# A residual block of two 3x3 convolutions: x's planes by negation and accumulating DMAs, conv 2's difference plane in rounded passes

## The reference

```python
identity = x
out = jax.nn.relu(_bn(_conv3x3(x, w1, stride=1), g1, b1, m1, v1))
out = _bn(_conv3x3(out, w2, stride=1), g2, b2, m2, v2)
return jax.nn.relu(out + identity)
```

## Time and profile before

| what | value |
|---|---|
| median of 3 runs | 596.51 us (595.66 to 597.7) |
| profiled execution | 596.25 us |
| its span, first to last instruction | 594.3 us |
| mean granted clock of TensorE | 0.994 of full speed |
| busy: TensorE, VectorE, ScalarE, POOL | 97%, 93%, 80%, 3% |
| DMA | 53.23 MB, mean 90 GB/s |
| one load of x, one store | 814 KB, 4.3 us to landing; 392 KB, 2.8 us |

### The profile page before, as it was taken

How to read it: one execution, slowest core, us unless ns; L and a number is a source line. 1 busy time by engine, 2 the same in 40 slices (tenths; PEclk the granted TensorE clock), 3 DMA queues, 4 the chain that set the end, 5 groups by cost and what they waited for, 6 DMA issues and landing times.

```text
span 594.3 us, 8667 instructions
## 1 busy us (share of the span) xinstructions
PE 576.5 (97%) x2962; PEld 533.7 (90%) x2962; DVE 555.3 (93%) x475; ACT 472.6 (80%) x730; POOL 19.8 (3%) x28
## 2 busy tenths in 40 slices
PE   6769999999999999999999999999999999999997
PEld 3769999999999999999999999999999999999996
DVE  6899999999999999999999999999999999999963
ACT  5687888887788887788887778888778888778874
POOL 7500000000000000000000000000000000000000
PEclk9799999999999999999999999999999999999999
DMA  4112223322223331232332222332122233121012
GB/s 161 56 61 88 104 84 110 112 82 82 83 83 110 110 108 56 83 109 84 110 110 67 89 92 83 110 110 93 71 83 93 100 110 110 58 82 51 29 55 108
DMA packets 22458, 53.23 MB, mean 90 GB/s; under 512 B 1584, under 2 KB 18096, under 8 KB 22448
## 3 DMA queue, kind: packets, MB, share of 16 engines
q1 hardware_dynamic: 22304, 52.80, 25.0%
q10 hardware_dynamic: 144, 0.29, 0.2%
HBM read 27.40 MB, written 25.69 MB: 89 GB/s over the span
## 4 chain that ended last, share of the span: by engine, by line
PE 93%; DVE 2%; ACT 1%; issue 0%; POOL 0%
PE psum L639 93%; DVE x_outer L367 1%; DVE x_lo L375 1%; DVE psum L389 1%; ACT w_mat L488 0%; DVE t_outer L412 0%; POOL g_t L181 0%; ACT psum L514 0%; DVE t_inner L398 0%; DVE x_inner L355 0%; ACT out_sb L563 0%; ACT z L534 0%; ACT z L535 0%; DVE x_inner L359 0%
## 5 line engine op out<-in xcount | busy, mean ns | idle before, releaser
L639 PE MATMUL psum<-x_hi,w_hi 128*128 128x392 f32 (+2 forms) x512 | 175.3, 342 | 6.7 <-DVE x_lo L375 6.7
L639 PE MATMUL psum<-x_hi,w_lo 128*128 128x392 f32 (+2 forms) x512 | 175.8, 343 | 0.0
L639 PE MATMUL psum<-x_lo,w_hi 128*128 128x392 f32 (+2 forms) x512 | 175.1, 342 | 0.0
L389 DVE TENSOR_TENSOR psum<-psum,z 128x784 f32<-128x784 f32 (+1 forms) x128 | 127.1, 993 | 21.3 <-ACT hidden L540 9.9
L639 PEld LDWEIGHTS psum<-x_hi,w_hi 128*128 128x128 f32 x512 | 97.0, 189 | 8.3 <-issue 4.8
L639 PEld LDWEIGHTS psum<-x_hi,w_lo 128*128 128x128 f32 x512 | 97.0, 189 | 0.4
L639 PE MATMUL psum<-t_inner,w_mat 128*128 128x392 f32 x256 | 94.7, 492 | 2.7 <-ACT psum L514 2.7
L639 PEld LDWEIGHTS psum<-x_lo,w_hi 128*128 128x128 f32 x512 | 97.0, 189 | 0.4
L563 ACT ACTIVATE out_sb<-psum 128x784 f32<-128x784 f32 x64 | 52.8, 825 | 47.1 <-PE psum L639 47.0
L639 PE MATMUL psum<-h_lo,w_hi 128*128 128x392 f32 x256 | 87.3, 341 | 0.0
L639 PE MATMUL psum<-h_hi,w_hi 128*128 128x392 f32 x256 | 87.2, 341 | 0.0
(11 more groups left out here) (67 smaller groups left out, 747.5 us busy)
## 6 DMA issues: line engine op xcount, KB each, us to landing
x_sb<-x_dram SPq DMA_DIRECT2D x32, 814.0 KB, 4.3
out_dram<-out_sb SPq DMA_DIRECT2D x64, 392.0 KB, 2.8
w_raw<-w_dram ACTq DMA_DIRECT2D x1, 288.0 KB, 3.5
w_raw<-w_dram SPq DMA_DIRECT2D x1, 288.0 KB, 5.4
bn<-params_dram SPq DMA_DIRECT2D x1, 132.0 KB, 3.7
```

The source lines that it names most:

```text
L389: nc.vector.tensor_tensor(psum[:, half, EVEN:ODD + 1, 0:width], t1, z[:, half, :, 0:width], ALU.add).then_inc(joined[conv], 1)
L639: ins = nc.tensor.matmul(psum[:, half, bank, first:first + (j1 - j0) * WQ], w[:, i, far, :], moving, start=not onto and at == 0, stop=at = ...
```

## The change

- **Planes of x.** VectorE no longer adds and subtracts planes of x. `negate_x(s + 2)` writes minus the even columns into the second inner plane, and minus the columns one further into both outer planes, as two `tensor_scalar` instructions, two images ahead. A plain DMA (`load_even`) puts the even columns in the first inner plane. POOL issues two accumulating DMAs an image, which add x from DRAM: the odd columns to both inner planes (`add_inner`), the other operand to the outer planes (`add_outer`). The planes keep the padding column (29 columns a row instead of 28: 812 elements a plane), `x_outer` has two buffers, and x is loaded two steps further ahead.
- **Conv 2's difference plane** is split like the others: `split_hidden("inner", ...)` and `high_hidden("inner", ...)` now take both inner planes (1624 elements instead of 812), and its products are three rounded passes. TensorE waits for `hlo_ready["inner"]` ahead of both inner products, where it waited for the raw difference plane ahead of the first.
- **Zero rows** above and below x's planes are gone; conv 1's matmuls leave them out as before. The scratch of the filters lies in `z` and `out_sb`.
- The loop of steps is one turn shorter, and more steps stand outside it.

```diff
+            def load_even(n, k):
+                sp.dma_start(x_inner[:, k, 0], x_rows[n][:, 0:RUN]).then_inc(even_in[k], 16)
...
             def step(s, k):
-                if not isinstance(s, int) or s + 2 < N:
-                    wait(sp, tx_ready["outer"], s + 3 - XBUFS)
-                    load(sp, s + 2, k + 2)
+                if not isinstance(s, int) or s + 4 < N:
+                    wait(sp, negated["outer"], s + 3)
+                    load(sp, s + 4, k + 4)
                 if there_is(s, s - 2):
                     store(s - 2, 0)
                     store(s - 2, 1)
+                if not isinstance(s, int) or 0 <= s < N - 3:
+                    wait(sp, res_ready, 2 * s)
+                    load_even(s + 3, (k + 3) % 4)
...
+            def add_inner(n, k):
+                pool.wait_ge(even_in[k], (n - k) * (16 // TBUFS) + 16)
+                pool.wait_ge(negated["inner"], n + 1)
+                odd = x_rows[n][:, XPLANE + 1:XPLANE + 1 + RUN].unsqueeze(1).broadcast_to((P, 2, RUN))
+                pool.dma_start(x_inner[:, k], odd, accum_op=ALU.add).then_inc(tx_ready["inner"][k % 2], 16)
+
+            def add_outer(n, k):
+                pool.wait_ge(negated["outer"], n + 1)
+                pool.dma_start(x_outer[:, k % 2], runs(x_rows[n], 0, XPLANE),
+                               accum_op=ALU.add).then_inc(tx_ready["outer"][k % 2], 16)
+
+            add_inner(0, 0)
+            add_outer(0, 0)
...
             scale_matrix(pool, "all2")
-            low_weights(pool, "all2")
+
+            def step(s, k):
+                if is_step(s, 0):
+                    low_weights(pool, "all2")
+                if there_is(s, s + 2):
+                    add_inner(s + 2, (k + 2) % 4)
+                    add_outer(s + 2, (k + 2) % 4)
...
+            def negate_x(n, k):
+                dve.wait_ge(x_in[k % XBUFS], until(n, k))
+                wait(dve, res_ready, 2 * (n - TBUFS) + 2)
+                cells = x_sb[:, k % XBUFS]
+                nc.vector.tensor_scalar(x_inner[:, k, 1], cells[:, 0:RUN], -1.0, None,
+                                        ALU.mult).then_inc(negated["inner"], 1)
+                wait(dve, xlo_ready["outer"], n - 1)
+                nc.vector.tensor_scalar(x_outer[:, k % 2], runs(cells, 1, XPLANE), -1.0, None,
+                                        ALU.mult).then_inc(negated["outer"], 1)
+
+            negate_x(0, 0)
...
-                if ahead:
-                    sum_x(s + 1, ka)
-                if last:
-                    split_hidden("t1", s - 1, kl % 2)
-                if ahead:
-                    difference_x(s + 1, ka)
+                if there_is(s, s + 2):
+                    negate_x(s + 2, (k + 2) % 4)
+                if last:
+                    split_hidden("inner", s - 1, kl % 2)
                 if now:
                     join(1, s, 1, (2, s - 2))
-                if ahead:
-                    outer_x(s + 1, ka)
                 if last:
                     split_hidden("outer", s - 1, kl % 2)
...
-                if (conv, i) == (2, 2):
-                    return ((t_inner[:, 1], wmat[2]),)
...
-                elif i == 1:
-                    hi, lo = t1_hi, t1_lo
+                elif i in (1, 2):
+                    hi, lo = ti_hi[:, i - 1], ti_lo[:, i - 1]
...
-                pe.wait_ge(th_ready["t2"], n + 1 + more)
+                pe.wait_ge(hlo_ready["inner"], n + 1 + more)
                 pe.wait_ge(res_ready, 2 * n + half + 1)
                 sum_products(2, half, 2, SUM_T2, passes_of(2, 2, 0), True).then_inc(inner[2], 1)
-
-                pe.wait_ge(hlo_ready["t1"], n + 1 + more)
                 sum_products(2, half, 1, SUM_T1, passes_of(2, 1, 0), True).then_inc(inner[2], 1)
```

More of the change, by code:

```diff
@@ L65, in residual_block, with scratch @@
         out_sb = sb("out_sb", [P, 2, 2, (NQ // 2) * WQ])
-        w_raw = {1: sb("w1_raw", [P, 3, 3, C]), 2: sb("w2_raw", [P, 3, 3, C])}
+        spare = {1: z[:].rearrange("p h s r -> p (h s r)"), 2: out_sb[:].rearrange("p h s r -> p (h s r)")}
+        def scratch(conv, at, kinds):
+            size = kinds * 3 * C
+            return spare[conv][:, at:at + size].rearrange("p (k h c) -> p k h c", k=kinds, h=3)
+        w_raw = {conv: scratch(conv, 0, 3) for conv in (1, 2)}
         bn = sb("bn", [P, 8 + 4 * C])
@@ L75, in residual_block @@
         bias = sb("bias", [P, 2])
[L76 to L77 removed]
+        g_t = {conv: scratch(conv, 9 * C, 4) for conv in (1, 2)}
+        g_sum = {conv: scratch(conv, 21 * C, 1)[:, 0] for conv in (1, 2)}
         wmat = {1: sb("w1_mat", [P, 4, 2, P]), 2: sb("w2_mat", [P, 4, 2, P])}
@@ L144, in run @@
                 step(s, s % 4)
-            with eng.Fori(0, (N - 4) // 4) as turn:
+            with eng.Fori(0, (N - 8) // 4) as turn:
                 for k in range(4):
                     step(turn * 4 + (2 + k), (2 + k) % 4)
-            for s in range(N - 2, N + 2):
+            for s in range(N - 6, N + 2):
                 step(s, s % 4)
@@ L230, in newton_step, with runs, until @@
             after(eng.tensor_tensor(inv[:, part], inv[:, part], tmp[:, part], ALU.mult))
[L232 to L238, removed]
+        def runs(cells, first, step):
+            return cells[:, first:first + 2 * step].rearrange("p (s r) -> p s r", s=2)[:, :, 0:RUN]
         def x_full(which, k):
-            full, places = (x_outer[:], slice(0, 2)) if which == "outer" else (x_inner[:, k], slice(2, 4))
-            return full.rearrange("p s j q -> p s (j q)"), places
+            full, places = (x_outer[:, k % 2], slice(0, 2)) if which == "outer" else (x_inner[:, k], slice(2, 4))
+            return full.rearrange("p s (j c) -> p s j c", c=WQ + 1)[:, :, :, 0:WQ], places
         def x_part(t, k, places):
-            return t[:, k % 2, places, 1:NQ + 1, :].rearrange("p s j q -> p s (j q)")
+            return t[:, k % 2, places]
+        def until(n, k):
+            return (n - k % 2) * 8 + 16
         def hidden_rows(half):
@@ L254, in hidden_parts @@
             rows = hidden_rows(half)
-            if which == "t1":
-                return t_inner[:, 0, rows], t1_hi[:, rows], t1_lo[:, rows]
+            if which == "inner":
+                return t_inner[:, :, rows], ti_hi[:, :, rows], ti_lo[:, :, rows]
             return t_outer[:, :, rows], h_hi[:, b, :, rows], h_lo[:, b, :, rows]
@@ L298, in _ @@
             nc.gpsimd.memset(wmat[1][:], 0.0).then_inc(mat_zeroed, 1)
-            for t in (x_hi, x_lo):
-                for b in range(2):
-                    for row in (0, NQ + 1):
-                        nc.gpsimd.memset(t[:, b, :, row, :].bitcast(F32), 0.0).then_inc(zeroed, 1)
             nc.gpsimd.memset(hidden[:], 0.0).then_inc(zeroed, 1)
             nc.gpsimd.memset(wmat[2][:], 0.0).then_inc(mat_zeroed, 1)
+            def add_inner(n, k):
[9 more added lines that the diff above has]
+            add_outer(0, 0)
             after, row = chain(pool, bn_step[2]), slice(2 + C, 2 + 2 * C)
@@ L522, in high_hidden @@
                 act.wait_ge(th_ready[which], n + 1 + (half or 0))
-                wait(act, *((inner[2], 4 * n) if which == "t1" else (outer[2], 2 * (n - 1))))
+                wait(act, *((inner[2], 4 * n) if which == "inner" else (outer[2], 2 * (n - 1))))
                 nc.scalar.activation(hi, full, ACT.Copy).then_inc(hhi_ready[which], 1)
```

83 lines of the change are left out of this document (41 added, 42 removed).

## The result

| | before | after |
|---|---|---|
| median of the runs beside each other | 596.09 us | **697.66 us** |
| profiled execution, span | 596.25, 594.3 us | 698.68, 697.0 us |
| mean granted clock of TensorE | 0.994 | 0.933 |
| DMA | 53.23 MB, 90 GB/s | 119.82 MB, 172 GB/s |

The ratio is 1.1687 (95% interval 1.1643 to 1.1731). The forecast was 656.5 us with a range of 638 to 699: the sign is right, the median lies just inside the range, and 40 us are missing from the sum. They have two causes, the start and TensorE's clock, and neither is in the term that the prediction worked on hardest.

The account below looks back on a forecast made before the run. It took TensorE's matmuls to bound the kernel before. Span 594.3 + 57.6 (ring) + 3.7 (start) - 1.0 (end) = 654.6 us; with 1.95 around the span and a correction to the median, 656.5 us, range 638 to 699.

Parts of the forecast that it names:

- Matmuls: Conv 2's difference plane: six rounded slots replace two true fp32 products in each half, saving 0.24 us, 0.48 us a step.
- The ring: TensorE, ReLU, VectorE, TensorE: conv 2 waits 2.38 us a step for both inner low parts; +57.6 us in all.
- Negations: VectorE's two negations ahead of the inner split handle two elements at a time: 0.50 and 0.91, together 1.41 us.
- Rival 2: VectorE's negations run at one element a cycle: 1.26 us more a step, 38 us in all, 694 us; chance 0.10.
- Rival 3: POOL's accumulate issue and VectorE's outer negation hold each other up: 2.0 us a step, 60 us more, 717 us; chance 0.10.
- Start: Image 1's accumulates land at 29.8 us; conv 2 begins at 42.7 instead of 39.03: +3.7 us (0 to 7).
- DMA: Plain and accumulating loads need 15.1 of a step's 19.5 us even at twice the plain price for accumulates: costed at nothing.
- Rival 4: Accumulates so slow that DMA engines bound the step; at four times the plain price 24.4 us, about 800; chance 0.06.
- Stores: SyncE's stores stand behind a wait for the negation, but the output buffer is needed a whole step later: nothing.
- End: The last step's splits are done before TensorE asks, so two images' matmul savings stand: -1.0 us.
- Rival 1: TensorE's matmuls stay the bound if the low parts come within 8.57 us of the step's start: 585 us; chance 0.06.
- the step of 19.54 us: The loop's period: 10.95 us from conv 1's to conv 2's inner products, then 8.59; 19.54 for 17.64, in 30 intervals.

Follow-up runs that it names:

- e10: e9 with SyncE issuing an image's first store ahead of the wait for the next load; 586.94 us, ratio 0.9857 to the kernel before.
- e3: The kernel before with only conv 2's difference plane in three rounded passes, x's planes still by VectorE's sums and differences; 639.03 us, ratio 1.0713.
- e4: The changed kernel with conv 2's difference plane again as one true fp32 pass, so only the planes' part of the change; 614.18 us, ratio 1.0299.
- e1: The changed kernel with VectorE's split of the inner hidden planes put ahead of the negations; 630.12 us, ratio 1.0568.
- e5: The changed kernel with 12 matmuls of 92 columns into unread PSUM columns where TensorE waits in each step; 671.13 us, ratio 1.1257.
- e2: e1 with ScalarE's output ReLU also moved ahead of the rounding of the inner hidden planes; 617.08 us, ratio 1.0361.
- e8: e2 with the planes of images 0 and 1 made by VectorE from x_sb, without accumulating DMAs; 599.58 us, ratio 1.005.
- e9: e8 with VectorE's hidden sum and difference ahead of the last join, and ScalarE's rounding ahead of the output ReLU again; 590.48 us, ratio 0.9904.

## Why the prediction was right, and where it was wrong

- **Matmuls, -0.48 us a step**: right. A rounded pair takes 1.06 us (six slots, 348.24 to 349.30), and e10's step comes within 0.06 to 0.23 us of 17.16.
- **The ring, +57.6 us**: right, in its mechanism and its size. The short steps are 19.48 to 19.57 us for 19.54; only 28 of the 30 intervals are such steps. TensorE's idle time reads 2.10 to 2.17 rather than 2.38, since a profile's modelled end of a matmul lies a little behind its slot. The rounded passes bring the wait (e3 has it, e4 does not), the order in front of the split sets its length (e1), and the DMAs have no part in it (e3 has none that accumulates).
- **Negations, 1.41 us**: right (0.49 + 0.91). Rival 2 fell. By the Trainium skill's "VectorE: DVE Perf Modes", section "Mode 2×_2P", such a form handles two elements a cycle; the trace agrees, with 812 elements in 0.57 us, where the two-source `TENSOR_TENSOR` of the earlier trace rows takes 1.00.
- **Rival 3, POOL and VectorE in each other's way**: it did not come. POOL's issue at 365.39 (1.20 us) overlaps the end of the outer negation, which takes 1.00, and the two issues run beside the split, which takes 1.84 as in the earlier trace rows. The Trainium skill's "SBUF — State Buffer", section "Who interferes with whom", would have one of them held for the other's whole length; between a negation and an issue in the loop, which overlap by only 0.3 us, the trace shows no such hold. At the start one inner negation (31.67 to 32.24) ran wholly inside the issue of 31.63 and took 0.57 us like all others; that issue took 1.76 us, and whether the negation made it longer is open.
- **Start, +3.7 us**: the step that failed, as a size. It was 19.0, outside my 0 to 7. I wrote "a load lands 4.3 us after issue", and took that for an accumulate; image 0's plane was rounded 13.5 us after its issue and image 1's 10.7 us. I had also shifted the end of POOL's filter work by 2 us, to 25.5, where it was 31.70: I had left out that ScalarE fills conv 2's matrix only behind the rounding of image 0's planes, and so behind their landing. That makes 12.5 of the 15.3 us that were missing. The other 2.8 lie behind TensorE's start on image 1: its outer accumulate landed 4.6 us behind the inner one, so that VectorE's outer split began at 48.44, 2.8 us after the inner one had ended. The nearest row had been a plain load on a quiet queue; two accumulates, the loads and the filters at once were the case at hand. The Trainium skill's "DMA: Bandwidth & Descriptors", section "Anatomy of one DMA — SWDGE (gpsimd) path", from which the estimate of 3.9 us came, gives less than any accumulate here took: the medians are 10.9 and 15.2 us, and the shortest in any run took 7.4.
- **The clock**: the term that was missing. Nothing in the prediction asked what a TensorE that stands still every step does to its own clock. It costs 27 us behind the first interval, of which e5 gives back 25.5.
- **DMA, "I cost it at nothing"**: right in the steady state by its cover, and nearer to the edge than I thought. An accumulate takes 0.402 x 697.0 / 53.22 = 5.3 us of all engines for 1 MB, a plain one in the same run 0.308 x 697.0 / 66.11 = 3.2 (2.8 before). My bound was twice the plain price; the DMA share is 0.76 to 0.79 in a step, and 15.1 of 19.5 is 0.77. Rival 4 fell.
- **Stores, nothing**: right for the changed kernel, whose steps are long, but thin: they land after 11.4 us instead of 2.8, and when the ring is shorter (e2, e8, e9) ScalarE waits for them.
- **End, -1.0 us**: right, -0.9.
- **Rival 1, TensorE stays the bound**: fell for this order of instructions; e10 is that rival with another order.

So the range held the median by 2.4 us, and for reasons that it had not been drawn for: its upper end stood there for slower negations and for rival 3, which did not come. That the forecast held is luck; the step of 19.54 us is not.

## What to carry to other kernels

When work leaves an engine, look at where in its order it stood: what counts is what stands between the ring's two ends, not the engine's busy share. Price a wait that you add to TensorE at its length and, as with the 2.15 us here, at the slower products that can follow it, and if it can't be removed, ask whether reordering two instructions shortens it before anything else is tried. And take no landing time from a quiet queue for a start in which everything is loaded at once.

## What the chip showed that I had not expected

- TensorE's granted clock fell to its lower level for some 3.4 us behind 18 of 28 idle times of 2.10 to 2.17 us, one in each step, and behind the first interval never where the idle time of a step was 1.6 us (e3), 0.7 (e1), or 2.3 us of which 1.4 were filled with small matmuls (e5). Adding 12 useless matmuls a step made the kernel 25.5 us faster.
- Accumulating DMAs of fp32 from DRAM cost 1.6 times as much engine time per MB as the plain ones beside them (5.3 and 3.2 us), the same in e2, e4 and e10. Why is open.
- A store's landing time depended much on its place in SyncE's queue: with an image's first store issued ahead of the next load, in the same traffic, the median of the first stores fell from 9.8 us (e9) to 3.9 us (e10), and that of the second ones, still behind the load, from 14.2 to 10.9.
